# Reading a recurrent state with 64-row matmuls, two heads in two banks, in a fused attention and feed-forward kernel

## The reference, cut to what matters

```python
def _gla_scan(q, k, v, g):                 # one head: q, k, g (512, 64), v (512, 128)
    S0 = jnp.zeros((q.shape[-1], v.shape[-1]), q.dtype)
    def step(S, inp):
        qt, kt, vt, gt = inp
        S = jnp.exp(gt)[:, None] * S + kt[:, None] * vt[None, :]
        return (S, qt @ S)
    return jax.lax.scan(step, S0, (q, k, v, g))[1]
...
o = o * jax.lax.rsqrt(jnp.mean(o * o, axis=-1, keepdims=True) + EPS) * rms_w
o = o.reshape(b, t, DV) * jax.nn.silu(x @ Wg)
return o @ Wo
```

## Time and profile before

| what | us |
|---|---|
| three timed runs | 1316.63, 1316.76, 1313.33 |
| their median | 1316.63 |
| the profiled execution's own time | 1313.97 |
| its span, first to last instruction | 1312.2 |
| outside the span (1313.97 - 1312.2) | 1.8 |

### The profile page before, as it was taken

How to read it: one execution, slowest core, us unless ns; L and a number is a source line. 1 busy time by engine, 2 the same in 40 slices (tenths; PEclk the granted TensorE clock), 3 DMA queues, 4 the chain that set the end, 5 groups by cost and what they waited for, 6 DMA issues and landing times. The chain is left out here.

```text
span 1312.2 us, 23418 instructions
## 1 busy us (share of the span) xinstructions
PE 1230.2 (94%) x8372; PEld 1073.7 (82%) x8372; DVE 1044.8 (80%) x2404; ACT 711.3 (54%) x1443; POOL 635.0 (48%) x893
## 2 busy tenths in 40 slices
PE   5889999999999999999999999999999999999957
PEld 3677889888897888889888788988889888897956
DVE  3769788796978979787787978879697896978863
ACT  5365555656456465644756555565545646465423
POOL 5436353563445544564435635356354554456431
PEclk9989999999999999999999999999999999999988
DMA  3110010100101001010011001010010100100000
GB/s 97 38 33 17 17 49 1 54 17 17 49 21 49 1 17 49 21 49 1 17 49 53 16 17 49 1 54 16 17 49 21 48 2 17 49 21 33 1 17 17
DMA packets 31778, 38.27 MB, mean 29 GB/s; under 512 B 2448, under 2 KB 29104, under 8 KB 31664
## 3 DMA queue, kind: packets, MB, share of 16 engines
q1 hardware_dynamic: 31136, 36.25, 8.3%
q10 hardware_dynamic: 528, 0.52, 0.1%
HBM read 28.38 MB, written 8.39 MB: 28 GB/s over the span
## 5 line engine op out<-in xcount | busy, mean ns | idle before, releaser
L1047 POOL TENSOR_TENSOR k_decayed<-k_decayed,block_totals 128x256 f32<-128x256 f32 x192 | 168.2, 876 | 277.1 <-PE ps_level L298 276.6
L298 PEld LDWEIGHTS ps_level<-q_blockdiag,k_decayed 128*128 128x128 f32 x1792 | 227.1, 191 | 51.5 <-DVE q_blockdiag L585 41.1
L298 PE MATMUL ps_level<-q_blockdiag,k_decayed 128*128 128x128 f32 x1792 | 241.1, 278 | 26.4 <-DVE q_blockdiag L585 25.1
L575 DVE COPY_PREDICATED attn_T<-level_masks,ps_level 128x512 f32<-128x512 uint32 x160 | 152.7, 954 | 16.0 <-PE ps_level L298 16.0
L585 DVE TENSOR_TENSOR q_blockdiag<-q_blockdiag,block_totals 128x512 f32<-128x512 f32 x192 | 141.3, 736 | 28.1 <-PE ps_level L298 28.1
L1053 POOL TENSOR_TENSOR rstd<-rstd,minus_half 128x1 f32<-128x1 f32 x192 | 111.7, 584 | 106.6 <-DVE rstd L636 106.6
L255 PE MATMUL ps_big<-w_ff_hi,h_hi 128*128 128x256 f32 x512 | 150.1, 293 | 3.0 <-DVE h_lo L590 3.0
L257 PE MATMUL ps_big<-w_ff_hi,h_lo 128*128 128x256 f32 x512 | 144.8, 283 | 0.0
L256 PE MATMUL ps_big<-w_ff_lo,h_hi 128*128 128x256 f32 x512 | 144.7, 283 | 0.0
L837 ACT ACTIVATE gelu_out<-ps_big,ff_b_cols 128x512 f32<-128x512 f32 x128 | 88.0, 688 | 79.8 <-PE ps_big L257 43.2
L623 DVE SCALAR_TENSOR_TENSOR o<-o,o_rstd,out_gate 128x128 f32<-128x128 f32 x256 | 93.3, 426 | 45.0 <-POOL o_rstd L1068 45.0
(11 more groups left out here) (113 smaller groups left out, 3155.1 us busy)
## 6 DMA issues: line engine op xcount, KB each, us to landing
w_raw<-L_ffn_w SPq DMA_DIRECT2D x16, 1024.0 KB, 5.6
out<-y SPq DMA_DIRECT2D x16, 512.0 KB, 2.9
x_in<-L_attn_x SPq DMA_DIRECT2D x15, 512.0 KB, 3.9
ff_b_rows<-L_ffn_b SPq DMA_DIRECT2D x8, 128.0 KB, 2.6
x_in<-L_attn_x ACTq DMA_DIRECT2D x1, 512.0 KB, 4.0
w_raw<-L_attn_Wv SPq DMA_DIRECT2D x1, 512.0 KB, 6.0
w_raw<-L_attn_Wg SPq DMA_DIRECT2D x1, 512.0 KB, 7.1
y<-L_attn_Wo SPq DMA_DIRECT2D x1, 512.0 KB, 8.1
```

The lines of the kernel that those rows point to most:

```text
L298: last = nc.tensor.matmul(PL[tl][:, c * CH:(c + 1) * CH], kk[:, tl, c * CH:(c + 1) * CH], q[:, :, :, 1, :], start=True, stop=True)
L575: nc.vector.copy_predicated(dst, m.to_broadcast([P, 2 * NCH, HC // h, h]), src)\
L1047: nc.gpsimd.tensor_tensor(k, k, t.to_broadcast([P, n, h]), ALU.mult)\
```

## The change

The matmul with the queries and the state takes only the 64 rows of its head, for stationary and moving operand. The two heads of a pair now have different banks: head 0 of each pair is in `PO`, head 1 in `PS`, columns 0 to 255 of each. The new part of the state moves to columns 256 to 511 of `PS` (`D` is 256). Within a pair the order is now: `Am` of head 0, `Am` of head 1, then for c > 0 `qbd` with `S` of head 0 and of head 1. st(0) has one more wait, for the o_part operations of the sequence before. VectorE reads its operands from the new places.

```diff
                     elif C:
+                        pe.wait_ge(sem["dv_o"], at("dv_o", p, NCH * H))
                         pe.wait_ge(sem["dv_st"], at("dv_st", p, states(NCH - 1)))
                     for tl in range(KT):
                         for hh in range(2):
                             hd = 2 * tl + hh
-                            last = nc.tensor.matmul(PS[hh * HK:(hh + 1) * HK, tl * HV:(tl + 1) * HV],
+                            last = nc.tensor.matmul(PS[hh * HK:(hh + 1) * HK, D + tl * HV:D + (tl + 1) * HV],
                                                     kT[:, c, hd * HK:(hd + 1) * HK],
                                                     v[:, c, hd * HV:(hd + 1) * HV], start=True, stop=True)
...
-                    for hd in range(H):
-                        tl, hh = hd // 2, hd % 2
-                        w = slice(hd * HV, (hd + 1) * HV)
-                        last = nc.tensor.matmul(PO[:, w], Am[:, tl, 2 * c + hh, :], v[:, c, w],
-                                                start=True, stop=(c == 0))
-                        if c:
-                            last = nc.tensor.matmul(PO[:, w], qbd[:, tl, hh, c * CH:(c + 1) * CH],
-                                                    S[:, tl, :], start=False, stop=True)
+                    for tl in range(KT):
+                        w = slice(tl * HV, (tl + 1) * HV)
+                        for hh in range(2):
+                            hd = 2 * tl + hh
+                            last = nc.tensor.matmul((PO, PS)[hh][:, w], Am[:, tl, 2 * c + hh, :],
+                                                    v[:, c, hd * HV:(hd + 1) * HV], start=True, stop=(c == 0))
+                        for hh in range(2 if c else 0):
+                            r = slice(hh * HK, (hh + 1) * HK)
+                            last = nc.tensor.matmul((PO, PS)[hh][:, w], qbd[r, tl, hh, c * CH:(c + 1) * CH],
+                                                    S[r, tl, :], start=False, stop=True)
...
                     for hd in range(H):
                         w = slice(hd * HV, (hd + 1) * HV)
+                        src = (PO, PS)[hd % 2][:, (hd // 2) * HV:(hd // 2 + 1) * HV]
                         nc.vector.scalar_tensor_tensor(o[:, c % 2, w], v[:, c, w], dg[:, c * H + hd:c * H + hd + 1],
-                                                       PO[:, w], ALU.mult, ALU.add).then_inc(sem["dv_o"], 1)
+                                                       src, ALU.mult, ALU.add).then_inc(sem["dv_o"], 1)
...
-                        nc.vector.tensor_copy(S[:, :, :], PS[:, 0:KT * HV].rearrange("p (k v) -> p k v", k=KT))\
+                        nc.vector.tensor_copy(S[:, :, :], PS[:, D:D + KT * HV].rearrange("p (k v) -> p k v", k=KT))\
...
-                                                           PS[:, tl * HV:(tl + 1) * HV], ALU.mult, ALU.add)\
+                                                           PS[:, D + tl * HV:D + (tl + 1) * HV], ALU.mult, ALU.add)\
```

## The result

The changed kernel takes 1326.93 us (median of four runs, 1324.92 to 1328.59), the kernel before 1316.37 (1313.33 to 1316.76). The ratio is 1.0079, 95% interval 1.0067 to 1.0091: 0.8% slower, 10.6 us by the medians.

The account below looks back on a forecast made before the run. TensorE, matmuls busy 94% of the span, was taken as the bound. 8 x 0.33 (j = 0) + 7 x 0.99 (j = 1) + 0.3 (sequence 15) = +9.9 us on 1313.97; forecast 1325 us, range 1312 to 1342.

Parts of the forecast that it names:

- Four changes at 0.195 against two pairs side by side: Each att with c > 0: four shape changes cost 0.78 us, two overlapping pairs save 0.446, sum +0.33 us.
- Where it lies: Per sequence: j = 0 pays only att(3), 0.33 us; j = 1 pays all three att, 0.99 us.
- The cover: ogt(1)'s 1.08 us wait for og(1) behind att(2) at j = 0 absorbs 0.66 us, falling to about 0.4.
- The rest at nothing: st, the new wait at st(0), VectorE's operations, banks and DMA: all near 0, at most 0.8 us for the wait.
- Sequence 15: Last sequence, with waits of 0.81 and 0.98 us next to att(1) and att(2): counted as 0.3 us.
- no overlap: Rival: the two heads' 64-row matmuls in att don't overlap, +0.78 us per att, 1342 us; chance 0.12.
- free changes: Rival: going to half height within att costs nothing, 0.446 us less per att, 1303 us; chance 0.18.
- the half price: Rival: a change of height in att costs 0.1 us, gain and price cancel, 1314 to 1318; chance 0.12.

Follow-up runs that it names:

- eight changes of height: Changed kernel with each head's 64-row matmul right behind its full-height one, so nothing overlaps: 1382.02 us, ratio 1.0498 to the kernel before.
- the best order of the small matmuls: Changed kernel with att's four 64-row state matmuls first, right behind st, then the four full-height ones: 1311.64 us, ratio 0.9965 to the kernel before.

## Why the prediction was right

**Four changes at 0.195 against two pairs side by side.** Forecast +0.33 us for each att, measured 0.98 / 3 = 0.33 by the steps with j = 1 and 0.32 to 0.34 in the timeline, with both parts by themselves: a change of height costs 0.191 us (eight changes of height), and the overlap is complete. The trace before had no change of height; the price came from the column shapes of st, with 0.056 us added for the wider load. That addition mattered: 0.17 would have given +0.23 for each att. The Trainium skill says in "TensorEngine Tiling (Array Packing)", section "Key Properties", that changing the tiling mode drains TensorE and changing the tile does not. The timeline agrees for rows as for columns: at each change of mode the next start is 0.1 us late and the one behind it 0.1 again, while a pair in two tiles of one mode starts 0.01 us apart. That the first 0.1 is the draining and the second the weight load that nothing hides fits both, but no run here separates them.

**Where it lies.** j = 0: 0.33 forecast, 0.33 measured. j = 1: 0.99 and 0.98. The cover, the 1.08 us wait, was shown by taking it away. The wait fell to 0.58 and not, as I wrote, to about 0.4: of the 0.66 us, the way out of the last 64-row matmul of att(2) falls into the wait itself, and og(1) ends at the same time as before counted from st(0) (557.73 - 543.77 = 13.96, and 563.13 - 549.16 = 13.97, for the ogt(1) that follows it).

**The rest at nothing.** Right, ratio 0.9997 for the banks, the order and the added wait.

**Sequence 15.** Here I counted 0.3 us. In the profiled executions it is more: from the st(0) of that sequence to the end it is 67.55 us before and 70.65 after, and the granted clock differs. In the 17.3 us from st(0) of sequence 15 on, TensorE's granted clock is 0.90 before (the number behind the brackets),

```profile
1244.70:1262.00 17.30, 13.55 (x103) 12.11 (x104) 10.79 (x36) 5.01 (x27) 5.94 (x10) 0.90 0.09 31
```

and 0.80 after:

```profile
1256.21:1273.51 17.30, 14.00 (x93) 11.43 (x94) 9.92 (x34) 5.14 (x27) 5.85 (x10) 0.80 0.09 31
```

In this sequence TensorE has idle stretches, and the clock is at its lower level (1.2 GHz) for part of what follows. How long differs from execution to execution: the run with the change at j = 0 only, which has the old matmuls in sequence 15, takes 68.7 us there at a mean granted clock of 0.85, the one at j = 1 only, which has the new ones, 68.9 at 0.85; the kernels before and after have 0.87 and 0.83. So at the same mean clock the new matmuls cost some 0.2 us in this sequence, where 0.3 was forecast. Whether they also make a longer stretch at the lower clock more likely stays open. The two profiled executions differ by 14.6 us in their spans: 1.3 ahead of the first st(0), 10.2 in the 15 steps, 3.1 in sequence 15. The median of the runs differs by 10.6, so most of the two ends belongs to these single executions.

Sum of the forecast 9.9; measured 10.6 by the medians, 0.8% where 0.75% was forecast. Of this, 9.5 was forecast for the 15 steps, and their medians give 8 x 0.33 + 7 x 0.98 = 9.5. That the total came so close is in part chance: the kernel's own runs spread over more than 3 us, and the stated range, 1312 to 1342, was much wider than the miss. The steps are what bears the account out. Of the rivals, no overlap (1342) and free changes (1303) are excluded by the timeline and by the run with eight changes, and the half price by the same run: 0.19, not 0.1.

## What to carry to other kernels

Halving the rows of a matmul and running two side by side gains half of the pair's time, 0.22 us here for fp32 with 128 columns, but each change between a full and a tiled shape costs about as much, 0.19 us. So collect tiled matmuls behind one change, and put them next to other tiled ones, even those tiled the other way: one pair between full-height matmuls lost 0.17 us here, two pairs about broke even (-0.06), and two pairs right behind st gained 0.25 by the same sum, which the steps bore out. Other sizes and types were not measured. And before shortening work ahead of a wait, ask what the wait is for: here moving one transpose behind one projection gained 0.9%, the best order of the small matmuls 0.35%.

## What the runs showed of the hardware that I had not expected

A change from one tiled shape to another, narrow columns to half rows, costs no more than one from narrow columns to the full array (0.59 and 0.58 us from st to the next start). And a wait can cost more than its idle time says: 1.08 us in the trace, 1.32 us gained when it went, and 1.31 us of longer att hidden by it in the run with eight changes. Of that, 1.25 are in the starts ahead of the transposes and 0.05 in the starts within them.
